# A sparse FFN kernel: seven of its blocks become half blocks of 64 rows, two experts to a block, with W2 as the stationary operand

## The reference

```python
gate_scores = jax.nn.softmax(x @ Wg + bg, axis=-1)
topk_scores, topk_idx = jax.lax.top_k(gate_scores, TOP_K)          # TOP_K = 2 of NUM_EXPERTS = 8
topk_scores = topk_scores / (jnp.sum(topk_scores, axis=-1, keepdims=True) + 1e-08)
...
for e in range(NUM_EXPERTS):
    h = jax.nn.gelu(x @ W1[e] + b1[e])                             # 256 -> 1024
    y = h @ W2[e] + b2[e]                                          # 1024 -> 256
    output = output + y * combine_w[..., e:e + 1]
```

## Time and profile before

| | us |
|---|---|
| median of 3 runs | 430.43 |
| the three runs | 425.68, 431.43, 430.43 |
| span of the profiled execution | 422.9 |
| time around the span, against the median | 7.5 |
| TensorE busy | 385.5 (91%) |
| VectorE busy | 318.1 (75%) |
| ScalarE busy | 217.8 (52%) |
| GpSimd busy | 186.6 (44%) |

### The profile page before, as it was taken

One profiled execution on the slowest core, in us unless ns is written; L12 is line 12 of the kernel. 1 busy time (PEld: TensorE's weight loads), 2 busy tenths in 40 slices (PEclk: granted clock), 3 DMA queues, 4 the chain that ended last, 5 costly groups with the idle time before them and its releaser, 6 DMA issues.

```text
span 422.9 us, 15170 instructions
## 1 busy us (share of the span) xinstructions
PE 385.5 (91%) x4834; PEld 300.9 (71%) x4834; DVE 318.1 (75%) x989; ACT 217.8 (52%) x587; POOL 186.6 (44%) x273
## 2 busy tenths in 40 slices
PE   4868999999999989999999999999999999999960
PEld 3746777766677777777787877877787777778740
DVE  6576998979888877854788989776777777777760
ACT  2445786767777756645384444444443444444420
POOL 3300267777776666554543333233233333333341
PEclk9997999999999999999999999999999999999995
DMA  8648867777788654237233563332332333333210
GB/s 278 135 118 253 241 198 231 221 232 207 231 239 231 189 196 139 91 78 250 64 54 66 95 121 52 52 49 36 51 45 40 47 45 47 45 53 47 28 15 0
DMA packets 73441, 50.88 MB, mean 120 GB/s; under 512 B 48400, under 2 KB 67472, under 8 KB 73232
## 3 DMA queue, kind: packets, MB, share of 16 engines
q1 hardware_dynamic: 66168, 41.44, 36.1%
q0 software_dynamic: 7152, 8.47, 11.8%
q10 hardware_dynamic: 48, 0.01, 0.0%
HBM read 28.52 MB, written 17.37 MB: 109 GB/s over the span
## 4 chain that ended last, share of the span: by engine, by line
PE 63%; DVE 14%; issue 7%; POOL 6%; DMA 5%; ACT 1%; SPq 1%; ACTq 0%; DVEq 0%; POOLq 0%
PE ps L1264 59%; POOL rs L569 3%; DVE mx L925 3%; DVE wts L910 3%; DMA out<-stage,row_id 2%; POOL rs L571 2%; DMA area<-qd 2%; PE ps L1408 2%; PE ps L1402 2%; DVE xn L855 1%; DMA area<-in_x 1%; PE ps L1423 1%; DVE area L1179 1%; DVE nbT L1069 1%; DVE st L974 1%
## 5 line engine op out<-in xcount | busy, mean ns | idle before, releaser
L1264 PEld LDWEIGHTS ps<-stage,wts 128*128 x1872 | 130.8, 98 | 40.5 <-issue 2.0
L1264 PE MATMUL ps<-stage,wts 128*128 128x128 f16 x1872 | 155.2, 219 | 1.3 <-issue 1.3
L1264 PE MATMUL ps<-wts,area 128*128 x624 | 150.3, 327 | 0.1
L808 ACT ACTIVATE area<-ps,late 128x128 f32<-128x128 f32 x312 | 89.1, 371 | 114.5 <-PE ps L1264 111.5
L628 POOL DMA_INDIRECT out<-stage,row_id x39 | 69.0, 1770 | 129.7 <-DVE stage L1212 74.6
L1264 PE MATMUL ps<-area 128*128 128x128 f16 (+5 forms) x784 | 61.2, 226 | 6.8 <-DMA area<-qd 3.8
L1177 DVE TENSOR_SCALAR area<-area 128x512 f16<-128x512 f32 x78 | 33.7, 432 | 42.7 <-ACT area L808 39.6
L925 DVE TENSOR_REDUCE mx<-ps 128x3 f32<-128x462 f32 (+1 forms) x96 | 53.3, 577 | 12.8 <-PE ps L1264 12.8
L1264 PEld LDWEIGHTS ps<-area 128*128 128x128 f16 (+1 forms) x784 | 45.4, 101 | 18.5 <-issue 7.8
L1179 DVE SCALAR_TENSOR_TENSOR area<-area 128x512 f16<-128x512 f32 x78 | 54.8, 702 | 2.7
L671 ACT ACTIVATE area<-ps 128x512 f32<-128x512 f32 x80 | 47.0, 601 | 17.3 <-PE ps L1264 14.5
(11 more groups left out here) (131 smaller groups left out, 413.4 us busy)
## 6 DMA issues: line engine op xcount, KB each, us to landing
stage<-in_w SPq DMA_DIRECT2D x32, 512.0 KB
area<-qd SPq DMA_DIRECT2D x16, 256.0 KB, 4.0
qd<-wts SPq DMA_DIRECT2D x48, 64.0 KB, 2.1
area<-in_x SPq DMA_DIRECT2D x16, 128.0 KB, 3.3
out<-area SPq DMA_DIRECT2D x16, 128.0 KB
xlist<-pad_rows SPq DMA_DIRECT2D x15, 130.0 KB, 3.7
area<-nbT SPq DMA_DIRECT2D x64, 1.0 KB
area<-in_b SPq DMA_DIRECT2D x1, 1024.0 KB, 8.7
```

Source lines behind the costliest of these rows:

```text
L808: last = nc.scalar.activation(h32[par][:, c * P:(c + 1) * P], h_ps[par][m][:, f * P:(f + 1) * P], ACT.Gelu_apprx_tanh, bias=b1T[:, ds(numb ...
L1264: return nc.tensor.matmul(out_, lhsT, rhs, start=start, stop=stop, skip_group_check=skip)
```

## The change

Blocks keep their pipeline, but there are 36 of them: 32 of 128 rows and four **mixed** blocks, t = 20, 23, 26 and 29, made of half blocks of 64 rows. The first three have two half blocks, which may be of different experts, the last has one. An *entry* is what the schedule gives a place to: 32 whole and 7 half ones, again 39.

In a mixed block the tokens move with 64 columns through each expert's weights, in the ups as in the downs. In the downs (`down_turned`) W2 is stationary and the hidden values move, so the result stands turned, with the 256 outputs on partitions. ACT adds b2 and writes it to SBUF (`y_out`), PE turns it back with two transposes (`turned_back`), and DVE has one operation (`weigh_turned`) in place of three, a step later than `weigh`. The downs follow as before three steps behind the ups. `load_block` issues both DMAs per entry, `add_block` an indirect DMA per entry; for two entries both go over 128 rows, of which 64 have a row number outside `out`. `load_block` now waits for `extract` of block t-8 in place of t-4. The phase 1 schedule on DVE has more operations (steps 14 to 27 of its loop in place of 15 to 23), with a table of constants that is loaded once (`s32`, 128 x 318).

```diff
-NBLK = (2 * B * NQ - E) // P + E
-SPARE = NBLK - 2 * B * NQ // P
+HP = P // 2
+NFULL = 2 * B * NQ // P
+NHALF = E - 1
+NBLK = NFULL + (NHALF + 1) // 2
+SPARE = (NHALF + 1) // 2
...
+LEFT = NFULL - K1
+MIXED = (K1 + 3, K1 + 6, K1 + 9, K1 + 12)
+ENTRIES = NFULL + NHALF
...
+        def entries(t):
+
+            if t in MIXED:
+                first = NFULL + 2 * MIXED.index(t)
+                return list(range(first, min(first + 2, ENTRIES)))
+            return [t - sum(j < t for j in MIXED)]
...
             def load_block(t):
-                _, (r,) = nc.values_load_multi_w_load_instructions(sched_i[0:1, 0, t:t + 1], engines=[sp.engine], min_val=0, max_val=XROWS - P,
-                                                                   skip_runtime_bounds_check_because="a block of a list or of the spare rows")
                 wait(sp, s.h_ps_d, 2 * (t - 3))
-                wait(sp, s.ex_d, t - 3)
-                sp.dma_start(xT[t % 4].rearrange("p (c t) -> p c t", c=4), xlist[ds(r, P), 0:D].bitcast(f16),
-                             transpose=True).then_inc(S[f"xt_in{t % 4}"], 16)
-                sp.dma_start(pay[t % 4].bitcast(i32), xlist[ds(r, P), D:ROW // 2]).then_inc(S[f"xt_in{t % 4}"], 16)
+                wait(sp, s.ex_d, t - 7)
+                for n, entry in enumerate(entries(t)):
+                    size = size_of(t)
+                    part = slice(n * size, (n + 1) * size)
+                    _, (r,) = nc.values_load_multi_w_load_instructions(
+                        sched_i[0:1, 0, entry:entry + 1], engines=[sp.engine], min_val=0, max_val=XROWS - size,
+                        skip_runtime_bounds_check_because="a block or half a block of a list, or of the spare rows")
+                    sp.dma_start(xT[t % 4].rearrange("p (c t) -> p c t", c=4)[:, :, part], xlist[ds(r, size), 0:D].bitcast(f16),
+                                 transpose=True).then_inc(S[f"xt_in{t % 4}"], 16)
+                    sp.dma_start(pay[t % 8][part].bitcast(i32), xlist[ds(r, size), D:ROW // 2]).then_inc(S[f"xt_in{t % 4}"], 16)
...
+            sp.wait_ge(s.pv_d, 4 * NT)
+            sp.dma_start(s32, s32_in).then_inc(s.s_in, 16)
...
             def add_block(t):
                 pool.wait_ge(s.y_done, t + 1)
-                wait(pool, s.added, 16 * t)
-                pool.indirect_dma_start(
-                    out=out_rows, out_offset=bass.IndirectOffsetOnAxis(ap=row_id[:, t % 4:t % 4 + 1], axis=0),
-                    in_=ysb[t % 2], in_offset=None, bounds_check=B * NQ - 1, oob_is_err=False,
-                    compute_op=ALU.add).then_inc(s.added, 16)
+                for n in range(len(entries(t))):
+                    wait(pool, s.added, adds(t) + 16 * n)
+                    pool.indirect_dma_start(
+                        out=out_rows, out_offset=bass.IndirectOffsetOnAxis(ap=row_id[tokens(t), t % 4, n:n + 1], axis=0),
+                        in_=ysb[t % 2][tokens(t)], in_offset=None, bounds_check=B * NQ - 1, oob_is_err=False,
+                        compute_op=ALU.add).then_inc(s.added, 16)
...
+                size = size_of(t)
                 for f in range(4):
-                    c = 4 * m + f
-                    last = nc.scalar.activation(h32[par][:, c * P:(c + 1) * P], h_ps[par][m][:, f * P:(f + 1) * P],
-                                                ACT.Gelu_apprx_tanh, bias=b1T[:, ds(number(e[t]) * FC + c, 1)], scale=1.0 / (SX * SW))
+                    for n, entry in enumerate(entries(t)):
+                        c, at_ = 4 * m + f, f * P + n * size
+                        last = nc.scalar.activation(h32[par][:, m * 512 + at_:m * 512 + at_ + size], h_ps[par][m][:, at_:at_ + size],
+                                                    ACT.Gelu_apprx_tanh, bias=b1T[:, ds(number(e[entry]) * FC + c, 1)],
+                                                    scale=1.0 / (SX * SW))
                 last.then_inc(s.h_done, 1)
+
+            def y_out(t, e):
+
+                par, i = t % 2, MIXED.index(t)
+                act.wait_ge(s.y_ps_d, t + 1)
+                wait(act, s.yt_back, i)
+                for n, entry in enumerate(entries(t)):
+                    for dc in range(DC):
+                        at_ = dc * P + n * HP
+                        nc.scalar.activation(yT[:, at_:at_ + HP], y_ps[par][:, at_:at_ + HP], ACT.Identity,
+                                             bias=b2T[:, ds(number(e[entry]) * DC + dc, 1)], scale=1.0 / (S_H * SW)).then_inc(s.yt_d, 1)
...
+                if k % 2 == 0 and k // 2 - 2 in MIXED:
+                    y_out(k // 2 - 2, e)
...
+            def weigh_turned(t):
+
+                par = t % 2
+                dve.wait_ge(s.yt_back, MIXED.index(t) + 1)
+                wait(dve, s.added, adds(t - 1))
+                dve.wait_ge(s.ex_d, t + 1)
+                dve.tensor_scalar(ysb[par][tokens(t)], y_ps[par][tokens(t), D:2 * D], wsel[tokens(t), t % 4, 0:1], None,
+                                  ALU.mult).then_inc(s.y_done, 1)
...
+                if k % 2 and (k - 5) // 2 in MIXED:
+                    weigh_turned((k - 5) // 2)
...
+            def evacuated(t):
+
+                if t > 0 and t - 1 in MIXED:
+                    pe.wait_ge(s.y_done, t)
+                else:
+                    wait(pe, s.yb_d, 2 * full_before(t))
+
             def up(k, f, w1e):
                 t, m, par = k // 2, k % 2, k // 2 % 2
 
                 if f == 0 and m == 0:
-                    pe.wait_ge(S[f"xt_in{t % 4}"], 32 * (t // 4 + 1))
+                    pe.wait_ge(S[f"xt_in{t % 4}"], loads(t))
                 if f == 0 and m == 1 and k >= 3:
-                    wait(pe, s.yb_d, 2 * ((k - 3) // 2 - 1))
-                c8 = 4 * m + f
-                for c in range(DC):
-                    for a, z in THREE:
-                        last = mm(h_ps[par][m][:, f * P:(f + 1) * P], w1e[:, a, c * F + c8 * P:c * F + (c8 + 1) * P],
-                                  xT[t % 4][:, (2 * z + c) * P:(2 * z + c + 1) * P],
-                                  c == 0 and (a, z) == (0, 0), c == 1 and (a, z) == (1, 0))
+                    evacuated((k - 3) // 2 - 1)
+                c8, size = 4 * m + f, size_of(t)
+                for n, w in enumerate(w1e):
+                    for c in range(DC):
+                        for a, z in THREE:
+                            x0 = (2 * z + c) * P + n * size
+                            last = mm(h_ps[par][m][:, f * P + n * size:f * P + (n + 1) * size], w[:, a, c * F + c8 * P:c * F + (c8 + 1) * P],
+                                      xT[t % 4][:, x0:x0 + size], c == 0 and (a, z) == (0, 0), c == 1 and (a, z) == (1, 0))
                 if f == 3:
                     last.then_inc(s.h_ps_d, 1)
+
+            def down_turned(k, f, w2e):
+
+                t, c, par = k // 2, 4 * (k % 2) + f, k // 2 % 2
+                if f == 0:
+                    pe.wait_ge(s.hh_lo, k + 1)
+                for n, w in enumerate(w2e):
+                    for dc in range(DC):
+                        for a, z in THREE:
+                            at_ = c * P + n * HP
+                            last = mm(y_ps[par][:, dc * P + n * HP:dc * P + (n + 1) * HP], w[:, (2 * c + a) * D + dc * P:(2 * c + a) * D + (dc + 1) * P],
+                                      hh_[par][:, z, at_:at_ + HP], (c, n, dc, a, z) == (0, 0, 0, 0, 0), c == FC - 1 and (a, z) == (1, 0), True)
+                if c == FC - 1:
+                    last.then_inc(s.y_ps_d, 1)
+
+            def turned_back(t):
+
+                par, n = t % 2, HP * len(entries(t))
+                pe.wait_ge(s.yt_d, adds_mixed(t))
+                for dc in range(DC):
+                    last = nc.tensor.transpose(y_ps[par][0:n, D + dc * P:D + (dc + 1) * P], yT[:, dc * P:dc * P + n], ident)
+                last.then_inc(s.yt_back, 1)
...
-                    if here:
-                        down(k - 3, f, w2e)
-
-                    if f == 1 and k % 2 and k // 2 + 1 in range(1, len(e)):
-                        pe.lower_val(e[k // 2 + 1][0])
+                    if here and (k - 3) // 2 in MIXED:
+                        down_turned(k - 3, f, w2e)
+                    elif here:
+                        down(k - 3, f, w2e[0])
+
+                    if f == 1 and k % 2 and k // 2 + 1 < NBLK and entries(k // 2 + 1)[-1] < len(e):
+                        for n in entries(k // 2 + 1):
+                            pe.lower_val(e[n][0])
+                if k % 2 and (k - 5) // 2 in MIXED:
+                    turned_back((k - 5) // 2)
```

More of the change, by code:

```diff
@@ L1182, in extract @@
             def extract(t):
-                slot = t % 4
-                dve.wait_ge(S[f"xt_in{slot}"], 32 * (t // 4 + 1))
+                slot, column = t % 4, expert_at(entries(t)[0])
+                dve.wait_ge(S[f"xt_in{slot}"], loads(t))
                 wait(dve, s.y_done, t - 3)
-                first, z, zsum = (pay[slot][:, n:n + 1] for n in (1, 2, 3))
```

(15 more changed lines are left out.)

248 lines of the change are left out of this document (173 added, 75 removed).

## The result

The changed kernel takes 451.25 us in the median of five runs (447.72 to 452.16), the kernel before 428.02 beside it (425.68 to 431.43): 1.058 times as long, 95% interval 1.0536 to 1.0625. The forecast was 454 (444 to 463). The profiled execution has a span of 445.8 us, 22.9 more than before.

The account below looks back on a forecast made before the run. PE's sequencer, paid per computed address, was taken as the bound. 19.8 + 1.0 + 0.6 + 2.5 = +23.9 us on a span of 422.9 gives 446.8; with 7.5 around it, 454.3, said as 454 us (444 to 463).

Parts of the forecast that it names:

- The bound: In the FFN, PE's sequencer needs 0.125 us for each computed address, with about 7% left in a normal group.
- Price of an address: On PE in mixed blocks' groups: 0.130 us per computed address, between 0.125 and 0.1346.
- the restart: Where PE resumes after reading its second set of registers, nothing queued: loads start 0.125 us apart, as register operations do.
- Blocks fewer, mixed blocks, block 29: PE's FFN time: three blocks fewer -16.2 us, three mixed blocks +33.2, block 29 +2.8; together +19.8, ends +16.7 and +22.6.
- Turning back: Four times two fp32 transposes on PE, 0.20 us each: 1.6 us at most, taken as 1.0.
- The wait behind it: PE waiting for `weigh_turned`: covered for blocks 20, 23 and 26, 0.6 us for block 29 (ends 0 and 1).
- The end: The last blocks' adds, now with real rows, follow at 4.7 to 5.1 us: +2.5 us (0 to 3.3).
- At nothing: Costs taken as zero: the adds' chain, covered by PE's sequencer; DVE's schedule (+4 us without cover); SP's loads; fewer spare pads.
- D: PE's clock falls to half speed around mixed blocks: +13 us on the sequencer-paced forecast, 467 us, chance 0.05.
- Rival B: On PE, address operations run ahead; mixed groups cost array time, adds bind: 422 us, between 415 and 425, chance 0.07.
- What would show it: Profile signs: x1728, groups of 1.17 and 1.56 us, short PE idle times, loads 0.125 us apart, POOL's adds waiting for DVE.

## Why the prediction was right, step by step

**The bound.** Right, and firmer than it was put. It left 7% to the sequencer in a normal group; in truth the sequencer was the pace there too (0.673 us against 0.660 with fixed addresses).

**Price of an address.** Taken at 0.130 us between 0.125 and 0.1346; it is 0.133 to 0.135 in the three stretches that it paces (half steps 39 to 57 of the kernel before, of the changed one, and of the one with more addresses). The doubt that part of 0.1346 was waiting for the array was unfounded: in mixed groups, in which the array has work for 0.7 of 1.2 to 1.6 us, an address costs as much. In the changed kernel 1,457 of the 1,727 distances between register operations are 0.124 to 0.125 us, as at the restart; the others, mostly 0.15 to 0.28, lift the mean. What stands in those was not taken apart.

**Blocks fewer, mixed blocks, block 29.** -16.2, +33.2 and +2.8 us were forecast, +19.8 together. Measured by the ends of the steps: -16.1, +35.0, and +3.3 for block 29 (5.26 less the 1.98 that went with the waits when the weighing came first). That is 22.2, near the upper of the two ends that were given (+22.6).

**Turning back.** 1.0 us forecast, nothing found: at the rate of the kernel before, 624 addresses x 0.1347 = 84.0 us are all of the 83.5 us, in which six of the eight transposes lie. No run takes the transposes out by themselves.

**The wait behind it.** The one step that failed in its reason. It was said that blocks 20, 23 and 26 are covered since the step between holds ups of a mixed block of two entries. Behind block 26 these are the ups of block 29, which has one entry, five addresses a group and so 2.6 us. PE's waits over 298 to 430 us in the changed kernel:

```profile
PE ps L1441 <- DVE stage L1361: 1.1, 2, 0.7
```

Two waits: 0.71 us idle behind block 26, where none was forecast, 0.43 behind block 29 (its two downs last until the next start 0.92 us in place of 0.33, so +0.6, as forecast). The place in the code, the weighing behind the split and the payload on DVE, was as described, and moving it took both away. Both together were worth 2.0 us, where 0.6 was forecast.

**The end.** +2.5 forecast, +2.56 measured, by the landings named.

**At nothing.** The adds: right in the changed kernel, where PE waits for none of them. Their price without that cover, put at "some 6 in all", is 4.9 to 6.0 us by the medians of the two kernels with both adds and one. PE waits for neither SP nor, beside the two waits above, DVE. PEclk has 9 in every slice of the FFN up to the end, so D didn't come. It came where PE did stand, 4.2 us in the kernel with fixed addresses.

**Rival B** was priced at 422 us with free addresses. The kernel with fixed ones is that case: 0.977 of the kernel before, 418 us from 428. What it had wrong for the changed kernel is that addresses are free.

**What would show it.** x1728, the two group lengths and the loads' pace came. "Short idle times of PE ... so a lower busy share" did not. The window that answers to the earlier trace rows:

```profile
325.00:350.00 25.00, 24.94 (x293) 19.41 (x291) 10.39 (x37) 6.98 (x28) 6.32 (x4) 1.00 0.22 31
```

PE is busy for 24.94 of 25.00 us with 293 matmuls, many of half the width, where it had 303 full ones. A matmul's recorded length (0.2 us) spans the 0.125 us to the next, so the gaps can't be seen. POOL's waits didn't turn wholly to DVE either: within a mixed block the second add waits for the first, and those of the whole blocks behind it wait for the add before.

**The total.** 454.3 against 451.25; by the medians +23.2 us for a forecast of +23.9. That this is so close is in part luck. The FFN's part grew by 25.8 us, 1.9 more than forecast (an address at 0.134 in place of 0.130 and the longer waits, less the turning back and 1.0 us of the whole blocks in half steps 0 to 39), and the attention happened to be 2.9 us shorter in the profiled execution. The 430.43 us from which the forecast counted was 2.4 above the 428.02 of the kernel before beside the result.

## What to carry to other kernels

Count the addresses that an engine's sequencer must compute, not only matmuls and columns: split the weights' users in two and the addresses double, though the array's time stays. A busy share of 100% does not tell array from sequencer; the number of register operations in a stretch over its length does, and a kernel with fixed addresses shows it in one run. Where a block is cut in half for the sake of its rows, ask what is paid per block, here addresses and adds, before counting the rows saved.

## What the runs showed of the hardware

- On PE a computed address took 0.133 to 0.135 us on average where it was the pace, whether matmuls of 64 or 128 columns followed, though the register operation itself is 46 ns. Most followed each other at 0.124 to 0.125 us.
- Behind groups that the array paced (0.98 us with six addresses, plain downs), the first two groups with nine addresses took 0.67 and 0.68 us, the array's time, and the later ones 1.1 to 1.3.
- Matmuls of 64 columns, each with its own load of 128 columns, started 0.029 us apart once their addresses were fixed, so loads recorded at 97 to 99 ns overlapped threefold.
- In the changed kernel a chained add started 3.3 to 4.5 us after one of a half block, and 4.6 to 5.1 us after one of a whole block.
- In a wait of PE of 4.2 us (fixed addresses) its granted clock fell to 0.50, the 1.2 GHz level; groups took 1.27 us there and 0.66 once it was 1.00 again. In the changed kernel, with waits of 0.71 and 0.43 us, it stayed at 1.00.
- The same attention code ended between 185.3 and 193.9 us in ten executions of different kernels. A whole-run ratio of kernels that differ only later carries that scatter.
